# Routed memory of a decoder layer: 1,024 weights per token from four rank-one terms a head and one 32x32 product per token, instead of eight masked outer products

## The reference

```python
q = (xn @ w_q.T).reshape(b, n, 2, h, kd).transpose(2, 0, 1, 3, 4)
sim = jnp.einsum('pbnhd,hkpd->pbnhk', q, keys)      # 2 sides, 8 heads, 32 keys
s, i = jax.lax.top_k(sim, k)                        # k = 8 on each side
all_scores = (sx[..., :, None] + sy[..., None, :]).reshape(b, n, h, k * k)
scores, pk = jax.lax.top_k(all_scores, k)           # the 8 best of 64 pairs
w_down = key_in[idx]; w_up = key_out[idx]
o = jnp.einsum('bnd,bnhkd->bnhk', inputs, w_down)
o = jax.nn.gelu(o, approximate=False) * jax.nn.softmax(scores, axis=-1)
return jnp.einsum('bnhk,bnhkd->bnd', o, w_up)
```

## Time and profile before

| | |
|---|---|
| median of 3 runs | 3413.17 us |
| the profiled execution | 3410.9 us, its span 3409.2 us |
| memory phase in the span | about 661 to 1853 us |
| busy in the span | PE 85%, DVE 78%, ACT 67%, POOL 43% |
| TensorE's granted clock, mean | 0.929 of 2.4 GHz |

### The profile page before, as it was taken

How to read it: one execution, slowest core, us unless ns; L and a number is a source line. 1 busy time by engine, 2 the same in 40 slices (tenths; PEclk the granted TensorE clock), 3 DMA queues, 4 the chain that set the end, 5 groups by cost and what they waited for, 6 DMA issues and landing times.

```text
span 3409.2 us, 74113 instructions
## 1 busy us (share of the span) xinstructions
PE 2896.7 (85%) x23818; PEld 2181.0 (64%) x23818; DVE 2663.1 (78%) x6179; ACT 2300.4 (67%) x3434; POOL 1478.7 (43%) x837
## 2 busy tenths in 40 slices
PE   3999828677777777777777999989998999999999
PEld 2666515466666666666665666656667777777776
DVE  7999897888888888888887999976667666666665
ACT  2777635477777777777776666656666777777776
POOL 1333350188888888888886232224432000000000
PEclk9999958689899888899898999999996999999999
DMA  4000000000000000000001000000000000000000
GB/s 141 0 0 0 13 0 1 0 1 0 0 0 0 0 0 0 0 0 0 0 0 50 1 0 0 0 6 16 15 13 0 1 1 13 0 12 0 0 12 13
DMA packets 28639, 26.43 MB, mean 8 GB/s; under 512 B 4256, under 2 KB 23456, under 8 KB 28448
## 3 DMA queue, kind: packets, MB, share of 16 engines
q1 hardware_dynamic: 28576, 25.63, 2.5%
HBM read 21.43 MB, written 4.19 MB: 8 GB/s over the span
## 4 chain that ended last, share of the span: by engine, by line
PE 58%; POOL 19%; issue 16%; DVE 4%; ACT 1%; DVEq 1%; POOLq 0%; DMA 0%; ACTq 0%; SPq 0%
POOL work L485 17%; PE ps L839 7%; PE ps L1125 4%; PE ps L862 4%; PE ps L877 4%; PE ps L1094 3%; PE ps L850 3%; PE ps L1096 3%; PE ps L1095 3%; PE ps L1127 3%; PE ps L1126 3%; PE ps L890 2%; POOL work L474 2%; PE ps L1113 2%; PE ps L919 2%
## 5 line engine op out<-in xcount | busy, mean ns | idle before, releaser
L485 POOL TENSOR_TENSOR work<-work 128x1024 f32<-128x1024 f32 x512 | 963.3, 1916 | 150.2 <-DVE work L1541 150.1
L1014 PE MATMUL ps<-consts_sb,work 128*128 128x128 f32 x4096 | 557.1, 287 | 278.2 <-DVE work L1541 273.5
L1541 DVE SCALAR_TENSOR_TENSOR work<-work,ps 128x1024 f32<-128x1024 f32 x512 | 636.9, 1275 | 107.3 <-ACT ps L665 103.3
L1014 PEld LDWEIGHTS ps<-consts_sb,work 128*128 128x128 f32 x4096 | 473.2, 146 | 339.0 <-DVE work L1541 339.0
L439 POOL TENSOR_TENSOR work<-work,consts_sb 128x1024 f32<-128x1024 f32 x192 | 365.3, 1903 | 726.9 <-ACT work L549 552.9
L665 ACT ACTIVATE ps<-work 128x1024 f32<-128x1024 f32 x512 | 567.1, 1116 | 165.7 <-DVE work L1541 107.0
L1680 DVE TENSOR_TENSOR h_low<-consts_sb,h_up 128x1024 fp32r<-128x1024 f32 x128 | 158.4, 1237 | 190.6 <-ACT h_up L740 190.6
L839 PE MATMUL ps<-work 128*128 128x512 f32 x512 | 259.7, 609 | 3.2 <-issue 0.4
L1125 PE MATMUL ps<-h_low,d_up 128*128 128x512 f32 x512 | 214.4, 419 | 0.5 <-DVE h_low L1680 0.5
L1094 PE MATMUL ps<-a_low,w_up 128*128 128x512 f32 x512 | 203.4, 397 | 2.0 <-DVE a_low L1655 2.0
L1023 PEld LDWEIGHTS ps<-w,work 128*128 128x128 f32 x1024 | 150.9, 234 | 82.0 <-DVE work L1549 43.8
(11 more groups left out here) (254 smaller groups left out, 6279.3 us busy)
## 6 DMA issues: line engine op xcount, KB each, us to landing
ctxT_all<-in_ctxT SPq DMA_DIRECT2D x1, 4096.0 KB, 12.9
work<-in_ctx SPq DMA_DIRECT2D x64, 64.0 KB, 1.8
out<-x_all SPq DMA_DIRECT2D x4, 1024.0 KB, 5.1
big<-in_up SPq DMA_DIRECT2D x1, 2048.0 KB, 8.3
consts_sb<-in_consts SPq DMA_DIRECT2D x1, 936.0 KB
w<-in_key_inT SPq DMA_DIRECT2D x1, 512.0 KB, 3.8
w<-in_key_out SPq DMA_DIRECT2D x1, 512.0 KB, 5.1
rows_sb<-in_rows SPq DMA_DIRECT2D x1, 384.0 KB
```

The lines of the kernel that those rows point to most:

```text
L485: pool.tensor_tensor(EE[:, h % HRING, :].rearrange("p (i j) -> p i j", i=NKEY), EX[:, T.u, a:a + NKEY].unsqueeze(2).to_broadcast([P, NKEY, ...
L1014: ins = pe.matmul(psG[:, c, :], WW[:, h % HRING, c * P:c * P + P], ident, is_transpose=True, start=h == 0 and c % 4 == 0, stop=h == PH - 1 ...
L1541: dve.scalar_tensor_tensor(out=WW[:, h % HRING, :], in0=EE[:, h % HRING, :], scalar=T8[:, T.u, h, TOPK - 1:TOPK], in1=psEP[h % 2], op0=ALU ...
```

## The change

The weights of one head can only be nonzero where one side's key is among that side's best two: a pair of ranks (3, 3) or deeper has at least 8 better pairs. So the head's 32 x 32 block of chosen weights is a sum of four rank-one terms: two one-hot vectors of the best and second key of side x times a vector over y, and two one-hot vectors of side y times a vector over the rest of x. With 8 heads this is, for each token, one product of a 32 x 32 matrix (32 terms by 32 keys x) with another (32 terms by 32 keys y).

- POOL: `candidates` makes 28 instead of 64 candidate pairs per head. `terms` makes the vectors (8 heads at once, 256 or 512 values an instruction), `ranks` the one-hot vectors. `outer` is gone.
- ACT: `shares` is 8 instructions of 4 x 32 values (the `for h` loop) in place of 8 of 1,024. `key_exps` is two instructions. One instruction ahead of the loop puts key_in into another order of experts (KI).
- DVE: `chosen` is 8 instructions of 4 x 32 values. `turn_sides` transposes both sides in 32 x 32 blocks, so that terms lie on partitions, and `turn_back` brings the result back to one token per partition.
- PE: `gates` (64 transposes a tile) is gone. `spread_heads` is 128 matmuls a tile of 32 rows, 32 weight columns and 32 moving columns, in turn on the four diagonal 32 x 32 positions of the array. `turn_weights` is 8 transposes.
- SP: key_out is loaded by four DMAs in the new order of experts.
- The order of the segments is new on all four engines, and `mixed` and `add_memory` have lag 3 instead of 2.

```diff
-            staggered(nc, pool, NT, [(1, outer(0, 6)), (0, best_pairs), (1, outer(6, PH))])
+            staggered(nc, pool, NT, [(0, candidates), (0, terms), (0, ranks)])
...
-                        act.activation(psEP[h % 2], EE[:, h % HRING, :], ACT.Copy, scale=RZ[:, T.u, h:h + 1]).then_inc(ep_ready, 1)
+            def shares(T):
+                u = T.u
+                act.wait_ge(rz_ready, T.now())
+                act.wait_ge(terms_ready, T.now())
+                need(act, xy_ready, T.before(1))
+                for h in range(PH):
+                    ins = act.activation(psSH[:, :, h, :], terms_of(u)[:, :, h, :], ACT.Copy, scale=RZ[:, u, h:h + 1])
+                ins.then_inc(share_ready, 1)
...
-            staggered(nc, act, NT, [(2, shares(0, 3)), (1, key_exps), (2, shares(3, 7)), (2, hidden), (0, normed), (2, shares(7, PH))])
+            staggered(nc, act, NT, [(0, normed), (1, shares), (0, key_exps), (1, hidden)])
...
-                            ins = pe.matmul(psG[:, c, :], WW[:, h % HRING, c * P:c * P + P], ident, is_transpose=True,
-                                            start=h == 0 and c % 4 == 0, stop=h == PH - 1, skip_group_check=True)
+            def spread_heads(T):
+
+                pe.wait_ge(sides_ready, T.now())
+                need(pe, back_ready, T.before(1))
+                pe.sem_inc(pe_seen, 1)
+                for n in range(BLOCK):
+                    for g in range(P // BLOCK):
+                        rows = slice(BLOCK * g, BLOCK * g + BLOCK)
+                        ins = pe.matmul(psW[rows, n // 16, :, n % 16], XT[rows, T.u, :, n], YT[rows, T.u, :, n], start=True, stop=True)
+                ins.then_inc(spread_done, 1)
+
+            def turn_weights(T):
+                pe.wait_ge(back_ready, T.now())
+                need(pe, hg_ready, T.before(1))
+                need(pe, y_used_m, T.before(1))
+                for c in range(CHUNKS):
+                    ins = pe.transpose(psG[:, c, :], WT[:, c * P:c * P + P], ident)
+                ins.then_inc(back_turned, 1)
...
-            staggered(nc, pe, NT, [(0, key_scores), (2, mixed), (1, gates(0, 2)), (1, hidden), (1, gates(2, PH))])
+            staggered(nc, pe, NT, [(0, key_scores), (2, spread_heads), (1, hidden), (3, mixed), (2, turn_weights)])
...
-                        dve.scalar_tensor_tensor(out=WW[:, h % HRING, :], in0=EE[:, h % HRING, :], scalar=T8[:, T.u, h, TOPK - 1:TOPK],
-                                                 in1=psEP[h % 2], op0=ALU.is_ge, op1=ALU.mult).then_inc(ww_ready, 1)
+            def turn_sides(T):
+
+                dve.wait_ge(xy_ready, T.now())
+                dve.wait_ge(hot_ready, T.now())
+                need(dve, spread_done, T.before(2))
+                dve.transpose(XT[:, T.u], x_side)
+                dve.transpose(YT[:, T.u], y_side).then_inc(sides_ready, 1)
+
+            def turn_back(T):
+
+                dve.wait_ge(spread_done, T.now())
+                need(dve, back_turned, T.before(1))
+                dve.transpose(WT, psW.rearrange("p q k t -> p k q t")).then_inc(back_ready, 1)
...
-            staggered(nc, dve, NT, [(1, chosen(0, 1)), (2, gated), (0, top_keys), (0, less_best), (1, chosen(1, 2)), (2, add_memory),
-                                    (1, chosen(2, 6)), (0, top_pairs), (0, pair_sums), (1, chosen(6, 7)), (0, pair_shares),
-                                    (1, chosen(7, PH))])
+            staggered(nc, dve, NT, [(0, top_keys), (0, less_best), (1, chosen), (2, turn_back), (0, top_pairs), (3, add_memory),
+                                    (1, turn_sides), (0, pair_sums), (2, gated), (0, pair_shares)])
```

More of the change, by code:

```diff
@@ L20 @@
 NKEY = 32
-HRING = 4
+BLOCK = 32
 PH = 8
@@ L400, in _ @@
             sp.dma_start(kin, key_inT).then_inc(tables, 16)
-            sp.dma_start(kout, key_out.rearrange("(c p) d -> p c d", p=P)).then_inc(tables, 16)
+            for j in range(P // NKEY):
+                sp.dma_start(kout[NKEY * j:NKEY * j + NKEY], key_out.rearrange("(a c j) d -> j a c d", a=NKEY, c=CHUNKS)[j])\
+                    .then_inc(tables, 16)
             sp.wait_ge(phase, PHASE["attn1"])
@@ L478, in outer @@
-            def outer(first, last):
-                def seg(T):
-                    pool.wait_ge(ex_ready, T.now())
-                    for h in range(first, last):
-                        a, b = NKEY * h, NKEY * (PH + h)
-                        need(pool, ww_ready, T.step(PH, h + 1 - HRING))
-                        pool.tensor_tensor(EE[:, h % HRING, :].rearrange("p (i j) -> p i j", i=NKEY),
-                                           EX[:, T.u, a:a + NKEY].unsqueeze(2).to_broadcast([P, NKEY, NKEY]),
-                                           EX[:, T.u, b:b + NKEY].unsqueeze(1).to_broadcast([P, NKEY, NKEY]),
-                                           ALU.mult).then_inc(ee_ready, 1)
-                return seg
@@ L647, in _ @@
             act.wait_ge(phase, PHASE["memory"])
+            act.wait_ge(tables, 16 * (1 + P // NKEY))
+            act.activation(KI.rearrange("p (j i) -> p i j", j=NKEY), kin.rearrange("p (i j) -> p i j", j=NKEY), ACT.Copy).then_inc(keys_turned, 1)
             def normed(T):
@@ L654, in key_exps @@
             def key_exps(T):
+                u = T.u
                 act.wait_ge(d_ready, T.now())
-                act.activation(EX[:, T.u, :], EX[:, T.u, :], ACT.Exp).then_inc(ex_ready, 1)
-            def shares(first, last):
-                def seg(T):
-                    act.wait_ge(rz_ready, T.now())
-                    for h in range(first, last):
-                        act.wait_ge(ee_ready, T.step(PH, h + 1))
-                        need(act, ww_ready, T.step(PH, h + 1 - 2))
-                        act.activation(psEP[h % 2], EE[:, h % HRING, :], ACT.Copy, scale=RZ[:, T.u, h:h + 1]).then_inc(ep_ready, 1)
-                return seg
+                first, y = EX[:, u, 0:BEST + NS], keys_of(u)[:, 1]
+                act.activation(first, first, ACT.Exp)
+                act.activation(y, y, ACT.Exp).then_inc(ex_ready, 1)
+            def shares(T):
+                u = T.u
+                act.wait_ge(rz_ready, T.now())
[4 more added lines that the diff above has]
+                ins.then_inc(share_ready, 1)
             def hidden(T):
+                need(act, hg_ready, T.before(2))
                 act.wait_ge(h_done, T.now())
-                need(act, hg_ready, T.before(1))
-                act.activation(HT, psH, ACT.Gelu).then_inc(h_ready, 1)
-            staggered(nc, act, NT, [(2, shares(0, 3)), (1, key_exps), (2, shares(3, 7)), (2, hidden), (0, normed), (2, shares(7, PH))])
+                act.activation(HT[:, T.u], psH, ACT.Gelu).then_inc(h_ready, 1)
+            staggered(nc, act, NT, [(0, normed), (1, shares), (0, key_exps), (1, hidden)])
             deviations(8)
@@ L988, in _ @@
             pe.wait_ge(phase, PHASE["memory"])
-            pe.wait_ge(tables, 32)
+            pe.wait_ge(tables, 16 * (1 + P // NKEY))
+            pe.wait_ge(keys_turned, 1)
             def key_scores(T):
```

133 lines of the change are left out of this document (90 added, 43 removed).

## The result

The changed kernel takes 3004.03 us (3000.69 to 3006.02, four runs) against 3413.35 us of the kernel before (3412.46 to 3416.44, four runs beside them): a ratio of 0.8798, 95% interval 0.8783 to 0.8814. Faster was right; the size was not. The forecast was 3204 us with a range from 3035 us on, and rival 1, at 3060 us, came nearest, yet it too was too slow.

A forecast was written before the change was run, and what follows sets the result against it. POOL was taken as the bound at 18.33 us a tile, and a PE-DVE loop of 15.0 us as the next: 63 periods save 210 us, KI costs 1 us, giving 3204 us as run median, range 3035 to 3365.

The forecast's parts named there:

- rival 1: Memory phase: small products cost 4 us or less, DVE and ACT close the loop; 3060 us, chance 26%.
- The bound before: Memory phase of the old kernel: POOL fullest, 16.4 of the 18.33 us period, with all four engines fairly full.
- the small product's price: PE's `spread_heads`: 256 instructions a tile at L877's pace of 0.0294 us each, 7.5 us.
- Its two ends: Limits for PE's small products a tile: 1.9 us if cost halves likewise again, 28.6 us at the 128-column price.
- rival 1's ring of 12.7 us: From DVE's reciprocal over `shares`, `chosen`, `turn_back`, top pairs, `add_memory`, transposes, sums, `gated` and back: 12.7 us.
- The ring: PE's small products, `hidden`, `mixed`, then DVE's `add_memory` and two transposes, back to the products: 15.0 us a tile.
- POOL stops being the bound at any of these: POOL's new work per tile put at 10.4 us, 9 to 13; at any of these POOL no longer bounds.
- Rival 2: DVE transposes each wait for a POOL instruction: 17.5 us a tile, 3361 us; chance 15% including like losses.
- Rival 3: PE's small products do not overlap: 15.0 us, period 22.5, 3676 us; chance 14% including the clock case.
- Its clock part: PE's clock falls to 0.50, doubling products, `hidden` and `mixed`: 26 us a tile, about 3900 us; chance 6%.
- PEclk near 1.00: Expected sign in the profile after: PE's granted clock stays near 1.00 in the memory phase.
- The ends of the phase: Start and end of the memory phase counted as equal despite the lag of 3; only KI adds 1 us.

The follow-up runs named there:

- before_half: The kernel before the change, with POOL computing only the first half of each outer product: 3324.39 us, ratio 0.9745.
- mixed_twice: The changed kernel with the output product `mixed` issued twice in a row: 3122.52 us, ratio 0.9152.
- p_dense: The changed kernel with the small products reading 32 neighbouring values instead of every 32nd, so the result differs: 3010.34 us, ratio 0.8821.
- layout: The changed kernel with DVE's transposes writing XT and YT so that products read neighbouring values, result unchanged: 3090.89 us, ratio 0.9059.
- keys_more: The changed kernel with the left half of the key-score product computed once more on PE: 2990.37 us, ratio 0.8770.
- ranks_warm: The changed kernel with the left half of the key scores computed once more and POOL's L540 reading a dense buffer: 2981.35 us, ratio 0.8741.
- p_onepos: The changed kernel with all 32 small products of one array position issued before the next position: 3772.40 us, ratio 1.1054.

## Why the prediction was right and wrong

**The bound before**: POOL, right, and before_half shows it. It also shows that POOL's relief alone was worth only 1.39 us a tile, since DVE and ACT were nearly as full; that PE had to lose work as well is not shown.

**The failed step: the small product's price.** "I take L877's pace: 256 x 0.0294 = 7.5 us." Measured: 3.85 us. The row was read rightly, but its unit was not the engine. L877 alternates between two positions, the new products between four, and the cost belongs to the position: 54, 28 and 14.3 ns an instruction on one, two and four. The prediction noted "four positions alternate instead of two" only as an argument for rival 1. Its two ends, 1.9 and 28.6 us, held the value; the centre was off by 3.65 us a tile, 63 x 3.65 = 230 us, more than the whole miss of 200 us. The Trainium skill's rule (TensorE: Matmul & The Clock Gate, Wait — 56ns, not 53.3ns?) that matmuls do not start less than about 25 ns apart would have given 6.4 us. The averages of 14.3 and 8.4 ns here contradict it.

That alone does not explain why the time fell below the range. With the price put right, the prediction's own sums lead to rival 1 and 3060 us, and the range began just below it, at 3035. The second step that failed is rival 1's ring of 12.7 us, below.

**The ring** came as forecast in its order, its members, and its size but for that term. 15.0 - 3.65 = 11.35 against 11.13 measured; hidden and mixed 3.84 where 3.90 and their handover were put, transposes with `add_memory` 3.04 where 3.24 were. mixed_twice shows that a ring through `mixed` takes 11.07 us. What the prediction missed is that a second ring, through the wait of `hidden` for L1577, is as long without the products and mostly closes last, so that a price below 3.8 us brings nothing: p_dense and layout show it.

**Rival 1** had the right price, "4 us or less", and took 12.7 us for the ring over `shares` and `chosen`. That ring is there too and ties with DVE's own row: `shares` ends at 1266.72 and DVE is done with `less_best` at 1266.79, so `chosen` waits for neither. But it takes 10.9 us: from start to start the reciprocal and `shares` are 2.67 (3.3 put), `chosen` 2.09 (2.4), `turn_back` 1.15 (1.24), `add_memory` to the reciprocal 4.19 (4.7). Each instruction in a row starts before the one ahead has ended, and prices of instructions taken singly add up to too much. With 11.1 us as the period rival 1's sum is 3410.9 - 63 x 7.23 + 3 = 2958 us; the longer ends (14) and the steps at 0.50 with the slow first tiles (63 x 0.52 = 33) bring it to 3005. The 0.52 us are the measured mean of 11.62 less 11.1, so that this last sum is bookkeeping and no second proof.

**POOL**: 10.4 us forecast, 10.5 busy (598 of 650 us over 57 tiles). With its waits for itself its row is 11.2 us, as keys_more shows, and it waits for hardly anything else. "POOL stops being the bound at any of these" was wrong by a hair: its row is as long as the steps at full clock. The operations on one tensor, for which there was no row, are 1.49 us for 512 values and 2.45 in place on a strided view, against 1.26 taken.

**ACT**: 8 x 0.30 = 2.4 us for `shares`, 3.0 forecast. It waits 200 of 650 us for L1594.

**Rival 2**, DVE and POOL in each other's way, did not come at its size: the transposes stay at 1.20 to 1.23 us beside a POOL that is always busy, as the Trainium skill (SBUF — State Buffer, Who interferes with whom) has it for one SBUF input. Only L1575, with two, has a mean of 403 ns instead of 291. The prediction gave it 0.6 us to spare; it lies on the second ring, where there is nothing to spare, and goes with the 0.1 us a step that keys_more and ranks_warm show.

**Rival 3**, no overlap: that is p_onepos, where the products took 14 us and the kernel 3772 us, slower than before. So 15.0 us and 3676 were a real danger, and the nesting of two loops kept from it. Its clock part came in small: steps with a stretch at 0.50 cost 0.9 us more, 13 in 52, and the first tiles run partly at 0.50 too. "PEclk near 1.00" was nearly right: 0.95 between 700 and 1400 us.

**The ends of the phase** were called equal; they cost 14 us. Part of it is in the last tile, where the products outside the loop wait for instructions:

```profile
1428.14 2.04 PE L1070 MATMUL ps<-work 32*32 32x32 f32 x128 [1.44 <-issue]
```

## What to carry to other kernels

When a price is read from a row of small matmuls, read also how many array positions take turns in it: what repeats is the price of one position, not the pace of the row, and both loop orders may give the right result while the products take four times as long in one. When the term that sets a ring is cut, look for the next ring that shares its other members (here `hidden`, `mixed`, `add_memory`) and closes through another wait, and take DVE's instructions by their starts in a row. When two engines touch the same memory, an instruction with a little room on its own engine can have none on the ring. Once PE waits in every period, less work on it can cost time through its clock, and a little useless work in a wait that is there anyway can give it back.

## What was not expected of the hardware

- A 32 x 32 fp32 product (two instructions) costs 54 ns an instruction in a row on one position, 28 on two in turn, 14.3 on four; on four with operands of neighbouring values 8.4.
- A loop body of some 1,200 PE instructions runs with 0.80 MB of instructions loaded over the whole program, one of 1,700 with 5.06 MB and gaps of 1.4 us before every block of 128 products.
- A DVE transpose of 1,024 fp32 values takes 1.20 to 1.23 us and 1.89 to 1.96 when it writes with a step.
- A POOL operation on one tensor of 512 values takes 1.49 us on a dense view in place, 1.94 from a dense view to a strided one, 2.45 on a strided view in place: more than the 1.08 of L519, which has two tensors.
- Leaving out half of the products made the kernel 110 us slower, with the granted clock at 0.50 in a part of every step.
- A DVE instruction of 128 values with both inputs in SBUF takes 0.39 us (median) beside POOL's L540 in place on a strided view, 0.29 us when that instruction reads a dense one.
